# Splitting the transfers of 111 rows into 96 and 15, and those of 34 rows into 32 and 2, in a nine-stage kernel on one core

## What is computed

```python
h = jnp.concatenate([tok(x), txt], axis=1)            # 8 x 333 x 256
h = h + attention_16_heads(ln(h))
h = h + gated_recurrence(ln(h))
h = h + rms_scan(ln(h))
h = h + quantised_mlp_3_blocks(ln(h))
h = h + masked_attention_1_head(ln(h))
h = h + top1_of_8_experts(ln(h)) 
h = h + alibi_attention_16_heads(ln(h))
h = h + capacity_8_experts(ln(h))
```

## Time and profile before

| | |
|---|---|
| median of 3 runs | 2174.61 us (2170.18 to 2179.5) |
| the profiled execution: its own time | 2175.37 us |
| its span | 2173.6 us |
| PE, DVE, ACT, POOL busy | 83%, 52%, 35%, 24% |
| mean granted clock of TensorE | 0.925 |
| moved by DMA | 153.89 MB, mean 71 GB/s |
| SP's queue (q1), GpSimd's (q0), ScalarE's (q10) | 124.40, 19.73, 8.13 MB |

### The profile page before, as it was taken

The page is one execution under the profiler, slowest core; times in us unless marked ns, Lnnn a source line. Parts: engine busy times, 40 slices in busy tenths (PEclk is TensorE's granted clock), DMA queues, the critical chain, the costliest instruction groups (busy, mean ns, idle before and its releaser), DMA issues. The chain is left out here.

```text
span 2173.6 us, 32276 instructions
## 1 busy us (share of the span) xinstructions
PE 1809.4 (83%) x9586; PEld 1192.9 (55%) x9586; DVE 1121.5 (52%) x3596; ACT 753.5 (35%) x1859; POOL 529.3 (24%) x719
## 2 busy tenths in 40 slices
PE   3299999997988899687858999478889999973998
PEld 3144444434665677555635666336666666652766
DVE  5277677764245766645442443346666666641111
ACT  1034444441321154222201111146665666621221
POOL 1110011003001122211122333123444444530122
PEclk9889999998997999899968999769999999976999
DMA  5454345509600000161111221130100000002341
GB/s 161 127 100 77 77 100 102 94 8 308 270 0 0 1 1 1 58 264 34 26 29 39 67 64 52 58 127 8 26 22 12 21 25 20 20 20 80 123 156 52
DMA packets 81760, 153.89 MB, mean 71 GB/s; under 512 B 23403, under 2 KB 65274, under 8 KB 77668
## 3 DMA queue, kind: packets, MB, share of 16 engines
q1 hardware_dynamic: 58586, 124.40, 19.8%
q0 software_dynamic: 19872, 19.73, 3.5%
q10 hardware_dynamic: 3161, 8.13, 1.5%
HBM read 90.78 MB, written 64.62 MB: 71 GB/s over the span
## 5 line engine op out<-in xcount | busy, mean ns | idle before, releaser
L2485 POOL TENSOR_SCALAR l_P<-l_P,l_ri 111x111 f32<-111x111 f32 (+1 forms) x256 | 177.5, 710 | 214.0 <-DVE l_ri L2654 213.7
L765 ACT ACTIVATE PT<-psT 111x666 f32<-111x666 f32 x192 | 139.3, 726 | 168.8 <-PE psT L863 168.2
L2744 ACT ACTIVATE l_P<-l_S,l_nm 111x111 f32<-111x111 f32 (+2 forms) x384 | 179.3, 471 | 35.9 <-DVE l_nm L2647 35.7
L662 DVE TENSOR_REDUCE mx<-psS 111x2 f32<-111x666 f32 x192 | 159.6, 848 | 31.5 <-PE psS L848 30.9
L874 PE MATMUL psO<-PT,vS 111*32 111x333 f32 x768 | 147.2, 462 | 0.1
L2864 PE MATMUL l_psP<-ident,l_P 111*111 111x111 f32 x768 | 105.2, 275 | 32.2 <-DVE l_PT L2663 26.1
L2864 PEld LDWEIGHTS l_psP<-ident,l_P 111*111 111x111 f32 x768 | 92.1, 183 | 63.2 <-issue 33.7
L2647 DVE CUSTOM_DVE_ANT_0 l_S<-l_psA,l_am 111x111 f32<-111x111 f32 (+1 forms) x256 | 79.1, 331 | 76.4 <-PE l_psA L2850 64.2
L2261 PE MATMUL t_psH<-expert_w,t_xT 128*128 x224 | 103.1, 605 | 1.6 <-DVE t_xT L2195 1.2
L2284 PE MATMUL t_psY<-expert_w,t_hT 128*128 x448 | 101.5, 380 | 0.7 <-DVE t_yb L2211 0.7
L2139 ACT ACTIVATE t_hg<-t_psH 128x512 f32<-128x512 f32 x56 | 33.4, 597 | 186.3 <-PE t_psH L2261 186.3
(11 more groups left out here) (420 smaller groups left out, 3732.8 us busy)
## 6 DMA issues: line engine op xcount, KB each, us to landing
xs_scratch<-zeros SPq DMA_DIRECT2D x30, 896.0 KB, 24.4
expert_w<-in_moe_dram SPq DMA_DIRECT2D x8, 2048.0 KB, 25.3
c_w<-in_moe_dram SPq DMA_DIRECT2D x16, 1024.0 KB, 7.4
qs<-halves_scratch SPq DMA_DIRECT2D x128, 83.5 KB, 3.2
ks<-halves_scratch SPq DMA_DIRECT2D x112, 83.5 KB, 4.0
halves_scratch<-high SPq DMA_DIRECT2D x32, 167.0 KB, 4.6
halves_scratch<-low SPq DMA_DIRECT2D x32, 167.0 KB, 4.8
c_xb<-xs_scratch SPq DMA_DIRECT2D x8, 667.3 KB
```

What stands on the lines that cost most here:

```text
L662: v.tensor_reduce(mx[J % 2][:, t, c:c + 65:64], psS[s % 2][0:TT, :, 0:T], AX.X, ALU.max, negate=True).then_inc(max_done, 1)
L765: s_.activation(PT[jp % 2][:, :, a, :], psT[0:TT, :, 0:T], ACT.Exp).then_inc(exp_done, 1)
L2485: r = g.tensor_scalar(Pt, Pt, ri[:, c % 2, 2 * t + half:2 * t + half + 1], None, ALU.mult)
L2744: s_.activation(P[c % 4][:, half, at(t):at(t + 1)], Sm[:, half, at(t):at(t + 1)], ACT.Exp, bias=nm[:, c % 2, i:i + 1], scale=-1.0, accum_o ...
```

## The change

A new helper, `send_rows`, sends rows 0 to 95 and rows 96 to 110 as two DMAs on one semaphore, which then counts 32 instead of 16 for a transfer. It takes the place of each plain transfer of 111 rows of the stream, of `rows`, of `l_xn`, of the plain results and of `c_xb`; the two of 34 rows become 32 and 2. In stage 7 the load of `h` also moves behind `fetch(1, 2)`. The two small broadcasts of 111 rows in stage 7 (L2436, L2442), the one of stage 5 and GpSimd's DMAs stay as they are.

```diff
+WIDE = 96
...
+def send_rows(eng, out, src, landed):
+
+
+    eng.dma_start(out[0:WIDE], src[0:WIDE]).then_inc(landed, 16)
+    eng.dma_start(out[WIDE:TT], src[WIDE:TT]).then_inc(landed, 16)
...
-            sync.dma_start(sh.h[:, 0:2, :], h0[0:2 * TT, :].rearrange("(t p) c -> p t c", p=TT)).then_inc(h_first, 16)
+            send_rows(sync, sh.h[:, 0:2, :], h0[0:2 * TT, :].rearrange("(t p) c -> p t c", p=TT), h_first)
...
-                sync.dma_start(sh.h[:, NT + t:NTILES:NT, :], later[t * TT:(t + 1) * TT]).then_inc(sh.h_rest, 16)
-            sync.wait_ge(sh.weights_in, 48)
+                send_rows(sync, sh.h[:, NT + t:NTILES:NT, :], later[t * TT:(t + 1) * TT], sh.h_rest)
+            sync.wait_ge(sh.weights_in, 64)
...
-            act.dma_start(sh.rows[:, :, :], ins["rows"].partition_broadcast(TT)).then_inc(sh.weights_in, 16)
+            send_rows(act, sh.rows[:, :, :], ins["rows"].partition_broadcast(TT), sh.weights_in)
...
-            act.dma_start(sh.h[0:IMG - 2 * TT, 2, :], h0[2 * TT:IMG, :]).then_inc(h_first, 16)
+            act.dma_start(sh.h[0:32, 2, :], h0[2 * TT:2 * TT + 32, :]).then_inc(h_first, 16)
+            act.dma_start(sh.h[32:IMG - 2 * TT, 2, :], h0[2 * TT + 32:IMG, :]).then_inc(h_first, 16)
...
-            dve.wait_ge(h_first, 32)
+            dve.wait_ge(h_first, 64)
...
-            dve.wait_ge(sh.h_rest, 48)
+            dve.wait_ge(sh.h_rest, 96)
...
-                sync.dma_start(routed.h[bass.ds(b * T, T), :].rearrange("(t p) c -> p t c", p=TT),
-                               sh.h[:, bass.ds(NT * b, NT), :]).then_inc(h_sent, 16)
+                send_rows(sync, routed.h[bass.ds(b * T, T), :].rearrange("(t p) c -> p t c", p=TT),
+                          sh.h[:, bass.ds(NT * b, NT), :], h_sent)
...
-                sync.dma_start(xn[:, :, :], routed.ys[bass.ds(b * T, T), D:2 * D].rearrange("(t p) c -> p t c", p=TT)
-                               ).then_inc(x_in, 16)
+                send_rows(sync, xn[:, :, :], routed.ys[bass.ds(b * T, T), D:2 * D].rearrange("(t p) c -> p t c", p=TT),
+                          x_in)
...
-            sync.dma_start(sh.h[:, :, :], routed.ys[:, 0:D].rearrange("(n p) c -> p n c", p=TT)).then_inc(h_in, 16)
             fetch(1, 2)
+            send_rows(sync, sh.h[:, :, :], routed.ys[:, 0:D].rearrange("(n p) c -> p n c", p=TT), h_in)
             stream.prefetch(sync)
...
-                sync.dma_start(out[bass.ds(b, 1)].rearrange("o (t p) c -> p (o t) c", p=TT), plain[:, :, :]
-                               ).then_inc(plain_sent, 16)
+                send_rows(sync, out[bass.ds(b, 1)].rearrange("o (t p) c -> p (o t) c", p=TT), plain[:, :, :], plain_sent)
...
-            dve.wait_ge(h_in, 16)
+            dve.wait_ge(h_in, 32)
...
-                    sync.dma_start(xb[p][:, :, :], xs[bass.ds(e * CAP, CAP), :].rearrange("(t p) c -> p t c", p=TT)).then_inc(x_in[p], 16)
+                    send_rows(sync, xb[p][:, :, :], xs[bass.ds(e * CAP, CAP), :].rearrange("(t p) c -> p t c", p=TT), x_in[p])
```

More of the change, by code:

```diff
@@ L266, in _ @@
             act.wait_ge(h0_first, 16)
-            act.dma_start(sh.h[0:IMG - 2 * TT, 2, :], h0[2 * TT:IMG, :]).then_inc(h_first, 16)
+            act.dma_start(sh.h[0:32, 2, :], h0[2 * TT:2 * TT + 32, :]).then_inc(h_first, 16)
+            act.dma_start(sh.h[32:IMG - 2 * TT, 2, :], h0[2 * TT + 32:IMG, :]).then_inc(h_first, 16)
             act.wait_ge(h0_rest, 16)
-            act.dma_start(sh.h[0:IMG - 2 * TT, NT + 2:NTILES:NT, :],
-                          h0[IMG:B * IMG, :].rearrange("(b q) c -> q b c", q=IMG)[2 * TT:IMG]).then_inc(sh.h_rest, 16)
+            last = h0[IMG:B * IMG, :].rearrange("(b q) c -> q b c", q=IMG)
+            act.dma_start(sh.h[0:32, NT + 2:NTILES:NT, :], last[2 * TT:2 * TT + 32]).then_inc(sh.h_rest, 16)
+            act.dma_start(sh.h[32:IMG - 2 * TT, NT + 2:NTILES:NT, :], last[2 * TT + 32:IMG]).then_inc(sh.h_rest, 16)
         @block.tensor
@@ L1677, in send @@
                 sync.wait_ge(stats_done, b + 1)
-                sync.dma_start(routed.h[bass.ds(b * T, T), :].rearrange("(t p) c -> p t c", p=TT),
-                               sh.h[:, bass.ds(NT * b, NT), :]).then_inc(h_sent, 16)
+                send_rows(sync, routed.h[bass.ds(b * T, T), :].rearrange("(t p) c -> p t c", p=TT),
+                          sh.h[:, bass.ds(NT * b, NT), :], h_sent)
             batches(sync, lambda b, p, first, last: send(b))
-            sync.wait_ge(h_sent, 16 * B)
+            sync.wait_ge(h_sent, 32 * B)
             for p in range(2):
@@ L2458, in _ @@
             send_plain(B - 1)
-            sync.wait_ge(plain_sent, 16 * B)
+            sync.wait_ge(plain_sent, 32 * B)
             sync.wait_ge(scattered, 16 * NT * B)
@@ L2499, in row_rest @@
                     pool.wait_ge(scattered, 16 * NT * b)
-                    pool.wait_ge(plain_sent, 16 * b)
+                    pool.wait_ge(plain_sent, 32 * b)
                 pool.wait_ge(row_ready, b + 1)
@@ L2802, in piece @@
                 if kind == "x" and j == 0:
-                    pe.wait_ge(x_in, 16 * b + 16)
+                    pe.wait_ge(x_in, 32 * b + 32)
                 if kind == "out" and j == 0:
@@ L3053, in turn @@
                 def turn(e, p, i):
-                    pe.wait_ge(x_in[p], 16 * (i + 1))
+                    pe.wait_ge(x_in[p], 32 * (i + 1))
                     pe.wait_ge(xT_ready, e)
```

## The result

| | before | after |
|---|---|---|
| median, runs side by side | 2172.39 us (2169.59 to 2179.5) | 2149.6 us (2140.14 to 2153.16) |
| ratio after / before | | 0.9883, 95% interval 0.9843 to 0.9924 |
| the profiled execution: its own time | 2175.37 us | 2149.58 us |
| its span | 2173.6 us | 2147.8 us |
| mean granted clock | 0.925 | 0.927 |

What follows compares the result with a forecast made beforehand. TensorE, busy 83% of the span, idles where 111-row transfers run on 3 of 16 DMA engines. Gains 10.7 + 1.4 + 2.5 + 4.0 + 8.3 = 26.9 us from 2175.4 or the median give 2148 us, range 2136 to 2162.

Steps and rivals of the forecast that it cites:

- That 111 rows run on 3 engines and 96 on 16: All split transfers: 111 rows use 3 of 16 DMA engines at 70 to 75 GB/s; 96 rows take the full width.
- Rival (a): The split widens nothing, or parts run one behind the other at the old pace: 2175 to 2187 us, 4%.
- Stage 0's end: SP's 14.29 us issue of two loads no longer holds the block's end; stage 1 starts 10.7 us earlier, bounds 7.7 and 12.
- Stage 1's start: Half stores land sooner, so ScalarE's first load and the first scores come 1.4 us earlier, bounds 0 and 3.
- With 4.8 it starts 1.4 earlier: Stage 1's start: with half stores landing in 4.8 us instead of 8.0, ScalarE's first load starts 1.4 us earlier.
- rival (c): Slower by the clock: 54 us more at granted clock 0.50 would eat the gain; 2183 us at 70, 2%.
- (d): Clock in favour: 10 to 20 us less low clock is worth 5 to 10 us, 2138 to 2143; below 2136 4%.
- Stage 7's start: Without the l_xn backlog, l_wo lands and VectorE's chain starts earlier: -2.5 us, bounds 0.4 slower and 3.
- `h`, -4.0 predicted: Stage 7: h on 16 engines lands about 1415, ending VectorE's wait for it; -4.0 us, bounds 3 and 4.5.
- Stage 8's start: Expert 0's rows and the biases arrive sooner, so the first layer starts 8.3 us earlier, bounds 6.0 and 9.6.
- biases as now: Stage 8's start, lower bound: the biases still hold VectorE's L3014 until 1987, giving 6.0 us instead of 8.3.
- Rival (b): Gates behind hold more, at several stage starts: 17 us in all, 2158; with one more 2162 to 2167; 20%.

Runs made afterwards that it cites:

- e5: Changed kernel with 111-row transfers split into 80 and 31 rows instead of 96 and 15; 2189.3 us, ratio to before 1.005.
- e12: Changed kernel with 111-row transfers split into 90 and 21 rows instead of 96 and 15; 2146.37 us, ratio to before 0.986.
- e6: Changed kernel with 111-row transfers split into 105 and 6 rows instead of 96 and 15; 2144.56 us, ratio to before 0.9853.
- e11: Changed kernel with 111-row transfers sent as 64, 32 and 15 rows instead of 96 and 15; 2148.32 us, ratio to before 0.9894.
- e1: Kernel before with only the loads into h_rest (seven later batches) split; 2162.3 us, ratio to before 0.9942.
- e8: Changed kernel with stage 8's two bias loads on separate semaphores and stage 7's angle and slope loads on ScalarE's queue; 2140.86 us, ratio to before 0.9834.
- e2: Kernel before with only stage 7 changed (fetches, h split and moved, plain results); 2171.57 us, ratio to before 0.9979.
- e10: Changed kernel with 105 and 6 rows, separate bias semaphores in stage 8, and stage 7's angle and slope loads on ScalarE's queue; 2143.08 us, ratio to before 0.9856.
- e3: Kernel before with only stage 8's row loads (c_xb) split; 2167.44 us, ratio to before 0.9973.
- e7: Changed kernel with stage 8's small and large bias loads on separate semaphores; 2147.87 us, ratio to before 0.986.

## Why the prediction was right, and where its steps were not

**That 111 rows run on 3 engines and 96 on 16** was the reading that carried all else, and it held as far as shares can show it: 0.20 to 0.98 with the same bytes. The width of 96 rows was a choice, taken over from transfers of 112 and 128 rows. Other divisors show in e5 (31 rows, 0.07), e12 (21 rows, 0.47) and e6 (6 rows, 0.41). Rival (a) fell by its pace, not by its order. The parts may well be served one behind the other: those of `h` land at 1408.3 and 1412.7 in after, and the three of e11 at 1404.5, 1408.6 and 1412.2. But nearly all engines work at each (a share of 1.12 in after and 1.11 in e11), where 3 did before (0.20).

**Stage 0's end, -10.7 predicted, -10.15 measured.** The image tokens' first store was issued at 54.0 instead of 53.3, so from there on the step gave 10.8. Every link is there: loads issued within 2 us, VectorE's statistics at 65.1 (64.4 predicted, and 0.7 for the late start), GpSimd done at 67.9 (67.1).

**Stage 1's start, -1.4 predicted, -6.4 measured**, outside the bounds of 0 to 3. The step that failed is "With 4.8 it starts 1.4 earlier": I took the median landing of the whole stage's 32 stores for that of an undisturbed one. It was no measure of this wait. In after the stores that the load waits for land in 2.6 us, and the next batch's, beside the loads of K and Q, in 6.2. ScalarE's load starts 2.7 us behind the store in after and 2.9 in e1. Nor were the 8.0 us of the earlier trace rows the landing of these stores: they belong to the next batch's, issued from 98.9 on, and for the first four the profile of before has none. Two things I didn't count at all were in the trace. SP's issue of the first store took 2.02 us in a full queue; it takes 0.35 now:

```profile
86.95 2.02 SPq L566 DMA_DIRECT2D halves_scratch<-high  x1
89.03 0.43 SPq L567 DMA_DIRECT2D halves_scratch<-low  x1
```

That is the kernel before. And ScalarE's sixteen loads, issued in 15.89 us, take 13.31 in after. The gain was no chance: from `xn` to the first scores it is 28.5 to 29.1 us in the four kernels with the loads of before, and 22.1 to 24.0 in the nine with wide ones (all but e5). The 6.4 are 1.0 until the last store's issue, 3.5 from there to ScalarE's load and 1.9 from that to the scores.

**Stages 1 to 6: 2.1 us lost, no term.** Their work is the same, and the same stretch takes between 1279.7 and 1292.4 us in the other twelve runs, so 2.1 is within what executions differ by. The sums by milestones fall by 2.2 us in the attention and 2.7 in the recurrence and come back by 2.2 before stage 6. Windows of 220 us of before and after around the second of these, shifted by the 14 us that separate them there:

```profile
480.00:700.00 220.00, 185.98 (x704) 125.05 (x701) 90.89 (x205) 52.96 (x97) 31.34 (x31) 0.91 0.40 143
```
```profile
466.00:686.00 220.00, 187.56 (x691) 125.95 (x692) 87.49 (x197) 52.17 (x96) 30.20 (x29) 0.88 0.40 143
```

The granted clock is 0.88 instead of 0.91, and 13 fewer matmuls fit. It is rival (c)'s mechanism, far from its price, and no more than what differs between executions. The low stretch at the start of stage 1 went the other way, as in (d): 30.7 us at 0.50 before, and in after a stretch as long with a mean of 0.63, followed by 0.99:

```profile
78.30:109.00 30.70, 18.45 (x72) 9.77 (x71) 17.92 (x41) 3.98 (x6) 5.02 (x10) 0.63 0.61 127
109.00:145.00 36.00, 34.21 (x219) 15.91 (x219) 27.30 (x78) 16.09 (x25) 7.79 (x9) 0.99 0.63 116
```

**Stage 7's start, -2.5 predicted, -1.4 measured.** The step that failed is the time of `l_wo` without the backlog, 2.2 us and "1.05 MB / 399 GB/s = 2.6 us". `l_xn` is in at 1379.12, so the backlog is gone, and `l_wo` still takes the 8.0 us of before. The DMA engines in after, from there on:

```profile
1380.00:1382.00 2.00, 0.00 (x0) 0.00 (x0) 0.00 (x0) 0.00 (x0) 0.00 (x0) 0.50 0.49 119
1382.00:1386.00 4.00, 0.00 (x0) 0.00 (x0) 0.00 (x0) 0.00 (x0) 0.00 (x0) 0.50 1.00 397
```

The weights flow at 397 GB/s only from 1382 on, 2.3 us after the last was issued at 1379.7: that pause is theirs, not `l_xn`'s. And nearly all 1.84 MB of them come then, 4.6 us at 399 GB/s, where I had counted only the 1.05 MB of `l_wo`. e8 shows that the pause isn't the place of the angles' broadcast either; what it is stays open. The 1.4 us came from the issues: from the fetch to `l_wo`'s issue it was 4.9 us and is 3.5. After's own start is a long one: in e2, e6 to e10 and e12 VectorE's chain starts 10.6 to 11.0 us after the fetch, 2.0 to 2.4 less than in before, and 11.5 in after. So the size was nearly right, by a mechanism that was not.

**`h`, -4.0 predicted.** VectorE's idle time fell by 4.1 (5.81 to 1.73), and the matmuls done in the 100 us after the first scores show about 4 us (under e2): the size was right. Its working was too good: from issue to landing I had 9 us, and the parts took 14.7 and 18.7, behind the second fetch and at 200 GB/s instead of 399. `h` was in at 1412.7 and the scores at 1419.6: 7 us of cover were left of the 19 I had. But that the 5.6 us up to stage 8 in the table are these 4 and the clock isn't shown: e1 and e3, without the change there, took 533.4 and 533.2 us for the stretch that takes 536.4 in after and 542.0 in before.

**Stage 8's start, -8.3 predicted, -4.3 measured**, outside the bounds of 6.0 to 9.6. The step that failed is "2.3 MB at 399 GB/s". The bytes were right (5 us at 207 GB/s and 6 us at 210 are 2.3 MB), the rate was half. Before, from 1979.0 to 1984.5, SP's queue with the rows had 0.16 of the engines' time and moved 0.27 MB, and GpSimd's with the biases 0.54 and 0.83 MB; now both experts' rows are on nearly all engines (0.99 from 1957 to 1962), and VectorE's L3023 starts 11.85 us after the rows' issue instead of 9.98. My lower bound "biases as now" left out that the change can make them later. e7 shows it: with the large bias off the gate, 5.0 us are won, 8.0 us from the issue to the first layer, and the predicted 9 us would have held. There was a row to warn of the rate: the kernel before moved 200 GB/s, at a share of 0.70, when rows and biases ran together there:

```profile
1979.00:1984.50 5.50, 0.00 (x0) 0.00 (x0) 0.00 (x0) 0.00 (x0) 0.17 (x1) 0.50 0.70 200
```

It also speaks against my reading that what was left of the biases shared three engines with `c_xb`: 200 GB/s is over twice what three give. The large bias has 111 rows but comes from GpSimd's queue, 888 KB in 8.8 us, 103 GB/s at the least, which is more than the 75 of three engines. Its queue's share of 0.54 in the stretch above is the time of 8.7 engines, so what 111 rows showed on SP's queue didn't hold for GpSimd's; how many engines it used the trace doesn't show.

**The sum** of 26.9 is nearer to the 25.8 than its steps are, and that is luck: 5.0 too little at stage 1 and 1.6 up to stage 8 stand against 4.0 too much at stage 8, 2.1 lost in stages 1 to 6, 1.1 at stage 7 and 0.6 at stage 0. By the medians the change gave 22.8 us. The forecast of 2148 missed by 1.6 and not by 4 because the median of before in the side-by-side runs, 2172.39, was 2.2 us under the 2174.61 that I started from. Rival (b), gates behind that hold more, was true of stages 7 and 8.

## What to carry to other kernels

Where a stretch shows a DMA share of 0.20 or 0.07 beside a queue that is never empty, look at the row count of the transfer. By their shares, 111 rows used 3 engines, 31 used one, and two transfers of 96 and 15 rows used nearly all. Count also what the full queue does to the engine that issues: here the 14.29 us issue that held a stage's end and the slow issues and landings after it were over half of the gain. When one transfer gets wide, ask what shares a semaphore or the DMA engines with it; a gate that counted a 32 KB load and an 888 KB load together cost 5 us that had not been visible before. And before a stage's length is read as the effect of an edit, look at its length in a run without the edit: stage 7 of before took 587.2 us in one kernel and 578.5 in two others.

## What the runs showed of the hardware that was not expected

- A share near 1 didn't mean 399 GB/s. From 2 to 9 us after the issue of `h` the 96-row part moved 213 GB/s in after, 220 in e2, 222 in e7 and 218 in e8, at shares of 1.09 and 1.10; the 1456 packets of after are 1.49 MB, 1 KB each. The rows of `c_xb` (2052 bytes each) moved 207 GB/s at 0.99 in after (1957 to 1962), and the weights 397 at 1.00 (1382 to 1386, 717 packets, of which the 126 of 8 KB and more carry 1.0 of 1.59 MB). The 105 rows of `h` moved 282 GB/s at 1.00 in e6 and 251 at 1.04 in e10.
- The same piece of 1 KB held an engine for longer when most engines were at work. Share x 16 engines x time / packets is 46 ns with 111 rows on three engines (before, 1403 to 1435: 0.204, 2267 packets), 85 ns with 96 rows (after, 1395.57 to 1402.57: 1.105, 1456 packets), 77 with 90 (e12, 1394.68 to 1401.68: 1.008, 1464) and 58 with 105 (e6, 1392.70 to 1399.70: 1.000, 1923).
- The weights of stage 7 flowed only about 2.3 us after the last was issued, in before (2.5 us, `l_xn` still under way, a share of 0.60 from 1395.5 to 1398.0) and in after (`l_xn` in, 0.49 from 1380 to 1382).
- Executions of one kernel lie 13 us apart: e11's four took 2142.14, 2142.63, 2154.01 and 2155.52 us at mean granted clocks of 0.930, 0.931, 0.926 and 0.926. A difference of 5 us between variants needs more than such times, and more than one trace of each.
